# Loading the table places of the supers on TensorE in fours inside the turn instead of sixteen at its head, in a GNN layer kernel

## The chip, the cores and the metric

The kernel runs on one core of one Trainium2 chip. The metric is the device time of one execution in microseconds (us). Engines are named as in the profile: PE is TensorE, DVE is VectorE, ACT is ScalarE, POOL is GpSimd, SP is SyncE, and a name with q (PEldq, SPq) is the sequencer of that engine, which runs register instructions, branches, loads into registers and DMA issues itself.

## The reference, cut to what matters

```python
sums = segment_sum(edge_attr, src, num_segments=n)            # 100000 edges x 64 features into 6250 nodes
counts = segment_sum(ones(edges), src, num_segments=n)
edge_attr_agg = sums / maximum(counts, 1.0)[:, None]
combined = concatenate([x, edge_attr_agg, u[batch]], axis=1)  # batch is all zeros
h = relu(combined @ W1 + b1)
x = layernorm(x + h @ W2 + b2)
```

## The kernel before, in words

The work has three stages. In the first, up to about 450 us, the edges are sorted: PE multiplies each batch of edges by permutation matrices that DVE builds (line 1146), ACT takes the result out of PSUM, and POOL scatters it by an indirect DMA (line 600) into `sorted_rows` in DRAM, grouped by bucket of nodes. Beside it runs the part of the first layer that needs only x.

The second stage, from 452 to 671 us, is the one that the change touches. The sorted rows are read back in 258 "supers" of 128 rows. Each super belongs to one bucket, and its 4 slots are added to that bucket's place in a table that fills all 8 PSUM banks. Per super PE does 24 matmuls (4 slots r, 2 halves h, 3 parts; line 936), each a 128x128 weight load of a one-hot matrix and 64 or 65 columns of data. DVE builds three one-hot matrices of an even super and four of an odd one (line 1236), ACT builds the fourth of the even ones (lines 713 and 716). SP loads the data of two supers with one DMA of 396 KB (line 511) into a ring of 8 pair buffers, once PE has finished with the buffer (`s_added`); it also loads x in 12 pieces (line 527). DVE and ACT write into 4 one-hot buffers, so they can be at most 4 supers ahead of PE; PE waits for them by `s_hot_d` and `s_hot_a` (lines 930 and 932).

Each engine runs its own loop over turns of BODY = 16 supers: 16 turns in a hardware loop (SUP_TURNS, line 942 on PE) and a last straight-line one of 2 supers (line 944). Where in PSUM a super belongs is known only at run time. DVE has computed it, and it lies as 32-bit integers in `where_row`, one row in SBUF: 384 places for PE, then 384 rows of `sorted_rows` for SP. PE's `super_turn` reads the 16 places of its turn into the registers `table_regs` with one load (line 927) at the head of each turn. `snap` (line 929) then turns a register into the address `at` of a super, and the matmuls of line 936 write to `at` and `at + 512`. SP does the same with its own 8 registers at the head of its turn (line 503). These sequencer instructions stand in the same order as the matmuls: PE's sequencer passes weight loads and matmuls on to the engine as it comes to them, and the engine works them off behind it.

The third stage, from 671 us, is the rest of both layers and the norm.

The functions around the change:

Of the kernel before, what the change touches and what calls it, by code (L numbers as in the profile page):

```python
# [9 lines left out]
I32 = mybir.dt.int32  # L10
# [7 lines left out]
P = 128  # L18
# [46 lines left out]
SUPER_PAIRS = -(-SUPERS // 2)  # L65
# [8 lines left out]
SUPER_COLS = -(-SUPERS // P)  # L74
# [20 lines left out]
HOT_BUFS = 4  # L95
BODY = 2 * PAIR_BUFS
SUP_TURNS = SUPER_PAIRS // PAIR_BUFS
ACT_SLOT = SLOTS - 1
TURN = 3
TURNS = CHUNKS // TURN  # L100
# [13 lines left out]
Z_BUFS = 3  # L114
assert X_TURN + X_PIECES + 1 == SUP_TURNS

# [6 lines left out]
def build(nc, x, src, attr, u, w1, b1, w2, b2, out):  # L123
# [12 lines left out]
    with ctx:  # L136
        def sb(name, shape, dt=F32):
            return ctx.enter_context(nc.sbuf_tensor(name, shape, dt))
# [7 lines left out]
        def sem(name):  # L146
            return ctx.enter_context(nc.semaphore(name))

        ident = sb("ident", [P, P])
        b2_all = sb("b2_all", [P, DIM])  # L150
        eps_col = sb("eps_col", [P, 1])
        where_row = sb("where_row", [1, 2 * SUPER_COLS * P], I32)
        node_of = sb("node_of", [P, 2 * P], I16)
        pre = sb("pre", [P, COLS * HID // P * NP])
        stats = sb("stats", [P, 2, 2, 6])
# [248 lines left out]
        def _(sp):  # L404
# [100 lines left out]
            def super_turn(m, count=PAIR_BUFS, found=False):  # L505
                if not found:
                    find_rows(m, count)
                for k in range(count):
                    at = sp.snap(row_regs[k], min_val=0, max_val=ZERO_SUPER * P)
                    sp.wait_ge(s_added, m * BODY + (2 * k + 2))  # L510
                    sp.dma_start(sup_pair[k][:, :, :, :].rearrange("p s r w -> p s (r w)"),
                                 sorted_rows[bass.ds(at, 2 * P), :].rearrange("(s p) w -> p s w", p=P)
                                 ).then_inc(s_sup[k], 16)
# [16 lines left out]
            for lo, hi in ((0, XPART), (XPART, NP)):  # L530
                sp.dma_start(xs[lo:hi, X_PIECES * X_PIECE:COLS * DIM], x_v[lo:hi, X_PIECES * X_PIECE:COLS * DIM]
                             ).then_inc(s_xs, 16)
            super_turn(SUP_TURNS, SUPER_PAIRS - SUP_TURNS * PAIR_BUFS)

# [103 lines left out]
        def _(act):  # L638
# [70 lines left out]
            def super_turn(m, count=BODY):  # L709
                for k in range(0, count, 2):  # L710
                    act.wait_ge(s_sup[k // 2], m * 16 + 16)
                    act.wait_ge(s_added, m * BODY + (k + 1 + SUP_FREE - HOT_BUFS))
                    nc.scalar.activation(apart[k // 2 % 2][:, :], node_of[:, :], ACT.Abs, scale=-1.0,  # L713
                                         bias=place_in[k][:, ACT_SLOT, :]).then_inc(s_apart, 1)
                    act.wait_ge(s_apart, m * PAIR_BUFS + (k // 2 + 1))
                    nc.scalar.activation(onehot[k % HOT_BUFS][:, ACT_SLOT, :], apart[k // 2 % 2][:, :], ACT.Relu, scale=-1.0,  # L716
                                         bias=1.0).then_inc(s_hot_a, 1)

            with act.Fori(0, SUP_TURNS) as m:
                super_turn(m)  # L720
            super_turn(SUP_TURNS, 2 * SUPER_PAIRS - SUP_TURNS * BODY)

# [46 lines left out]
        def _(pe):  # L769
# [153 lines left out]

            table_regs = [pe.alloc_register(f"table_reg{k}") for k in range(BODY)]

            def super_turn(m, count=BODY):
                pe.load(table_regs[0:count], where_row[0:1, bass.ds(m * BODY, count)])
                for k in range(count):
                    at = pe.snap(table_regs[k], min_val=0, max_val=(PAIR_BANKS - 1) * 1024 + (BANK_COLS - 1) * ROW)
                    pe.wait_ge(s_hot_d, m * BODY + (k + 1))  # L930
                    if k % 2 == 0:
                        pe.wait_ge(s_hot_a, m * PAIR_BUFS + (k // 2 + 1))
                    for r in range(SLOTS):
                        for h in range(2):
                            for part, width in ((0, FEAT), (1, FEAT), (2, ROW)):
                                last = nc.tensor.matmul(ps[:, bass.ds(at + h * 512, width)],  # L936
                                                        onehot[k % HOT_BUFS][:, r, h * P:(h + 1) * P],
                                                        sup[k][:, r, part * PLANE:part * PLANE + width],
                                                        start=False, stop=False)
                    last.then_inc(s_added, 1)  # L940

            with pe.Fori(0, SUP_TURNS) as m:
                super_turn(m)
            super_turn(SUP_TURNS, 2 * SUPER_PAIRS - SUP_TURNS * BODY)
            for k in range(BANKS):
                last = nc.tensor.matmul(table_p[k], zeros[:, :], zeros[:, 0:1].to_broadcast([P, table_p[k].shape[1]]),
# [408 lines left out]
```

## Time and profile before

| | us |
|---|---|
| median of 3 runs | 801.06 |
| lowest and highest | 800.24, 801.56 |
| span of the profiled execution, first to last instruction | 799.5 |
| PE busy / DVE busy / ACT busy in the span | 745.1 / 716.8 / 501.7 |

The page gives the span of the profiled execution and no device time of its own for it; the median lies 1.6 us above the span. The matmuls' ends are modelled by the profiler (a matmul of line 936 is shown as 193 ns long, while the next one starts 31 ns after it), so starts are the safer thing to read. A line of a source view gives kind, count, then duration in ns as min/median/max, then the start of the first and of the last one in us.

### The profile page before, as it was taken

The page shows a single profiled execution, that of the slowest core. Times are in us where ns is not written, and L with a number is a line of the kernel's source. Part 1 is how long each engine was busy: PE and PEld are TensorE (multiplying, and loading weights), DVE is VectorE, ACT ScalarE, POOL GpSimd, SP SyncE. Part 2 cuts the span into 40 slices and gives each one's busy share as a digit, 9 for nine tenths or more (in the row PEclk, how much of TensorE's full clock was granted, in tenths as well). Part 3 has the DMA queues.
Part 4 walks back from the last instruction along what each step waited for, and adds up shares of the span by engine and source line. Part 5 has one row for each costly group of instructions (what it writes and reads, how often), then busy time and mean ns, then how long its engine had stood idle before and what let it go on. Part 6 is the DMA issues. An engine that isn't in the chain of part 4 may idle for free.

```text
span 799.5 us, 31269 instructions
## 1 busy us (share of the span) xinstructions
PE 745.1 (93%) x11398; PEld 711.5 (89%) x11399; DVE 716.8 (90%) x2382; ACT 501.7 (63%) x998; POOL 417.1 (52%) x410
## 2 busy tenths in 40 slices
PE   8889999999999999999999888989898986899995
PEld 4689999999999999999999888989898986899995
DVE  8999999999999999999896388989898988799995
ACT  1366676666667767667667545555555552688886
POOL 3087777777677787877776400000000002788983
PEclk9999999999999999999999999999999999999999
DMA  6366556666665666656674678999999990012122
GB/s 215 131 210 204 201 202 211 213 215 219 202 219 195 212 220 211 225 205 214 203 210 167 239 227 260 281 282 282 285 283 285 281 277 10 27 52 64 53 66 64
DMA packets 75268, 156.38 MB, mean 196 GB/s; under 512 B 11084, under 2 KB 51277, under 8 KB 75097
## 3 DMA queue, kind: packets, MB, share of 16 engines
q1 hardware_dynamic: 58328, 102.33, 42.5%
q0 software_dynamic: 16896, 53.54, 17.9%
q8 instruction: 18, 0.29, 0.2%
q14 instruction: 26, 0.20, 0.1%
HBM read 95.47 MB, written 60.37 MB: 195 GB/s over the span
## 4 chain that ended last, share of the span: by engine, by line
PE 60%; DVE 30%; issue 5%; ACT 2%; POOL 1%; DMA 1%; DVEq 0%; ACTq 0%; SPq 0%; POOLq 0%
PE ps L858 33%; DVE onehot L1236 18%; PE ps L785 11%; PE ps L936 5%; PE ps L990 3%; DVE pre L1275 2%; DVE perm L1146 2%; DVE stats L1301 1%; DVE weights_z L1296 1%; PE ps L776 1%; PE ps L792 1%; POOL h_low L628 1%; PE ps L811 1%; PE ps L843 1%; PE ps L841 1%
## 5 line engine op out<-in xcount | busy, mean ns | idle before, releaser
L600 POOL DMA_INDIRECT sorted_rows<-payload,idx x264 | 304.8, 1155 | 131.8 <-issue 51.9
L858 PE MATMUL ps<-attr_buf,perm 128*128 128x198 bf16 x3168 | 302.6, 252 | 1.1 <-ACT attr_buf L642 0.8
L858 PEld LDWEIGHTS ps<-attr_buf,perm 128*128 128x128 bf16 x3168 | 288.6, 96 | 6.1 <-ACT attr_buf L642 1.2
L649 ACT CAST payload<-ps 128x792 bf16<-128x792 f32 x264 | 217.9, 825 | 76.7 <-PE ps L858 62.2
L1146 DVE TENSOR_SCALAR perm<-place_of,pos 128x512 bf16<-128x512 int16 x792 | 241.1, 362 | 3.4 <-PE ps L858 2.7
L1236 DVE TENSOR_SCALAR onehot<-node_of,sup 128x256 bf16<-128x256 int16 x903 | 192.4, 284 | 41.9 <-PE ps L936 22.3
L936 PE MATMUL ps<-sup,onehot 128*128 128x64 bf16 (+1 forms) x6192 | 196.1, 193 | 24.7 <-DVE onehot L1236 21.0
L936 PEld LDWEIGHTS ps<-sup,onehot 128*128 128x128 bf16 x6192 | 193.5, 98 | 27.3 <-issue 27.3
L619 POOL TENSOR_TENSOR xs<-xs,b_all 125x256 f32<-125x256 f32 x50 | 37.6, 775 | 209.4 <-DMA xs<-in_x 209.4
L713 ACT ACTIVATE apart<-node_of,sup 128x256 bf16<-128x256 int16 x129 | 65.6, 508 | 94.3 <-PE ps L936 90.2
L785 PE MATMUL ps<-xt,w1x 128*128 128x125 f32 x800 | 99.9, 278 | 5.9 <-DVE pos L1067 3.3
L785 PEld LDWEIGHTS ps<-xt,w1x 128*128 128x128 f32 x800 | 93.2, 192 | 10.8 <-issue 4.6
L660 ACT ACTIVATE pre<-ps,hid_bias 128x125 f32 (+1 forms) x200 | 56.7, 368 | 61.7 <-PE ps L785 61.7
L628 POOL TENSOR_TENSOR h_low<-pre,h_high 128x500 fp32r<-128x500 f32 x50 | 62.8, 1278 | 32.7 <-ACT pre L737 32.7
L1056 DVE TENSOR_TENSOR attr_buf<-attr_buf 128x576 f32<-128x576 f32 x88 | 65.8, 749 | 7.8 <-DMA attr_buf<-in_edge_attr 7.8
L1062 DVE TENSOR_TENSOR attr_buf<-attr_buf 128x576 f32<-128x576 f32 x88 | 65.4, 744 | 0.0
L716 ACT ACTIVATE onehot<-apart 128x256 bf16<-128x256 bf16 x129 | 53.8, 417 | 4.1
L990 PE MATMUL ps<-w_high,h_high 128*125 128x256 f32 x200 | 49.8, 282 | 1.0 <-issue 0.5
L990 PE MATMUL ps<-w_low,h_high 128*125 128x256 f32 x200 | 49.5, 280 | 0.0
L990 PE MATMUL ps<-w_high,h_low 128*125 128x256 f32 x200 | 34.1, 292 | 7.6 <-POOL h_low L628 7.6
L990 PEld LDWEIGHTS ps<-w_high,h_high 128*125 128x125 f32 x200 | 37.1, 185 | 1.3 <-issue 0.7
L990 PEld LDWEIGHTS ps<-w_low,h_high 128*125 128x125 f32 x200 | 37.2, 186 | 0.0
(150 smaller groups left out, 603.7 us busy)
## 6 DMA issues: line engine op xcount, KB each, us to landing
sup<-sorted_rows SPq DMA_DIRECT2D x129, 396.0 KB, 4.0
attr_buf<-in_edge_attr SPq DMA_DIRECT2D x43, 576.0 KB
out<-weights_z SPq DMA_DIRECT2D x25, 224.0 KB
xs<-in_x SPq DMA_DIRECT2D x12, 448.0 KB
x_stage<-in_x SPq DMA_DIRECT2D x47, 112.0 KB
sorted_rows<-payload,idx POOLq DMA_INDIRECT x264
pre<-jump_d SPq DMA_DIRECT2D x1, 1560.0 KB, 10.4
pre<-first_d SPq DMA_DIRECT2D x1, 780.0 KB, 7.2
```

The source lines that it names most:

```text
L600: pool.indirect_dma_start(out=sorted_rows, out_offset=bass.IndirectOffsetOnAxis(ap=idx[:, n:n + 1], axis=0), in_=payload[s][:, :], in_offs ...
L628: nc.gpsimd.tensor_tensor(h_r[b][1][:, at:end], pre[:, g * KH * NW + at:g * KH * NW + end], h_r[b][0][:, at:end].bitcast(F32), ALU.subtrac ...
L649: nc.scalar.copy(payload[s][:, :].rearrange("p (r w) -> p r w", w=PART), slots_p[s % PSUM_BUFS]).then_inc(s_pay, 1)
L713: nc.scalar.activation(apart[k // 2 % 2][:, :], node_of[:, :], ACT.Abs, scale=-1.0, bias=place_in[k][:, ACT_SLOT, :]).then_inc(s_apart, 1)
L785: last = nc.tensor.matmul(pre_p[b][:, k * NP:(k + 1) * NP], w1x[:, c, k * P:(k + 1) * P], xt[b][:, c, :], start=(c == 0), stop=(c == KX - 1))
L858: last = nc.tensor.matmul(slot_p[s % PSUM_BUFS][r].rearrange("p (h f) -> p h f", f=PLANE), places, parts(a, t * CB + s), start=(t == 0 and ...
L936: last = nc.tensor.matmul(ps[:, bass.ds(at + h * 512, width)], onehot[k % HOT_BUFS][:, r, h * P:(h + 1) * P], sup[k][:, r, part * PLANE:pa ...
L990: last = nc.tensor.matmul(y_p[b][0:NP, c * DIM:(c + 1) * DIM], h_r[b][part][:, at:at + NP], w2r[w_part][:, k * DIM:(k + 1) * DIM], start=( ...
L1056: nc.vector.tensor_tensor(left, whole, high, ALU.subtract).then_inc(s_rest, 1)
L1062: nc.vector.tensor_tensor(low, left, middle, ALU.subtract).then_inc(s_low, 1)
L1146: last = nc.vector.tensor_scalar(perm[s][:, t, :], place_of[:, :], pos[:, bass.ds(c * CT + (t * CB + s), 1)], None, ALU.is_equal)
L1236: last = nc.vector.tensor_scalar(onehot[k % HOT_BUFS][:, r, :], node_of[:, :], place_in[k][:, r, :], None, ALU.is_equal)
```

## The change

PE's 16 places of a turn are no longer read by one load at its head. A function `find_tables` reads 4 of them. Before the loop it is called once for supers 0 to 3. Within a turn of the loop it is called in supers 2, 6, 10 and 14, after the 6 matmuls of their first slot (r == 0), for the four supers that begin two supers later; the call in super 14 reads the first four of the next turn. The last straight-line turn of 2 supers has no load of its own: its places come with the last call in the loop. `where_row` is allocated first in SBUF instead of fourth, so that its address, and those of `ident`, `b2_all` and `eps_col`, are other ones. SP's loads are not changed.

```diff
+PLACES_AT_ONCE = 4
+assert 2 * SUPER_PAIRS - SUP_TURNS * BODY <= PLACES_AT_ONCE
...
+        where_row = sb("where_row", [1, 2 * SUPER_COLS * P], I32)
         ident = sb("ident", [P, P])
         b2_all = sb("b2_all", [P, DIM])
         eps_col = sb("eps_col", [P, 1])
-        where_row = sb("where_row", [1, 2 * SUPER_COLS * P], I32)
...
+            def find_tables(k, at):
+                pe.load(table_regs[k:k + PLACES_AT_ONCE], where_row[0:1, bass.ds(at, PLACES_AT_ONCE)])
+
             def super_turn(m, count=BODY):
-                pe.load(table_regs[0:count], where_row[0:1, bass.ds(m * BODY, count)])
                 for k in range(count):
                     at = pe.snap(table_regs[k], ...)
...
                                                         start=False, stop=False)
+                        if r == 0 and k % PLACES_AT_ONCE == 2 and count == BODY:
+                            following = k - 2 + PLACES_AT_ONCE
+                            find_tables(following % BODY, m * BODY + following)
                     last.then_inc(s_added, 1)
 
+            find_tables(0, 0)
             with pe.Fori(0, SUP_TURNS) as m:
                 super_turn(m)
             super_turn(SUP_TURNS, 2 * SUPER_PAIRS - SUP_TURNS * BODY)
```

## Rows read from the trace of the kernel before

**Rows 1.** The page: its span, and the chain that ended last

```profile
span 799.5 us, 31269 instructions
...
PE 60%; DVE 30%; issue 5%; ACT 2%; POOL 1%; DMA 1%; DVEq 0%; ACTq 0%; SPq 0%; POOLq 0%
```

**Rows 2.** Timeline of PE from 560 to 620 us: turns 8 to 12

```profile
start us, us, engine line op out<-in xcount [idle before <-releaser]
562.64 12.00 PE L936 MATMUL ps<-sup,onehot 128*128 128x64 bf16 x384 [1.30 <-DVE onehot L1236]
575.89 11.99 PE L936 MATMUL ps<-sup,onehot 128*128 128x64 bf16 x384 [1.25 <-DVE onehot L1236]
589.18 11.99 PE L936 MATMUL ps<-sup,onehot 128*128 128x64 bf16 x384 [1.29 <-DVE onehot L1236]
```

**Rows 3.** Busy time by engine in turns 8 and 9

```profile
core 0: us, PE busy (x) PEld busy (x) DVE busy (x) ACT busy (x) POOL busy (x), PEclk, DMA share, GB/s
562.64:575.89 13.25, 12.00 (x384) 11.88 (x385) 11.79 (x56) 7.41 (x16) 0.00 (x0) 1.00 0.95 284
575.89:589.18 13.29, 11.99 (x385) 11.88 (x385) 11.79 (x56) 7.40 (x16) 0.00 (x0) 1.00 0.91 283
```

**Rows 4.** Who waited for whom, 440 to 680 us, and SP's own waits

```profile
engine line waited for: us in total, times, longest us
ACT apart L713 <- PE ps L936: 90.2, 123, 2.4
DVE onehot L1236 <- PE ps L936: 22.3, 17, 1.4
PE ps L936 <- DVE onehot L1236: 21.0, 18, 1.3
PE ps L936 <- ACT onehot L716: 1.6, 1, 1.6
SPq L511 <- PE ps L936: 98.2, 110, 2.2
```

**Rows 5.** Sequencer rows at a turn's head, 573.9 to 576.2 us, by line

```profile
L942 PEldq ALU_OP  x1: 32/32/32, 573.9 to 573.9; - x1
L942 PEldq COMPARE_BRANCH  x1: 207/207/207, 574.0 to 574.0; - x1
L942 PEldq FUSED_REGOPS  x1: 65/65/65, 574.3 to 574.3; - x1
L927 PEldq TENSOR_LOAD <-where_row x1: 1106/1106/1106, 574.4 to 574.4; - x1
L929 PEldq FUSED_REGOPS  x2: 41/41/41, 575.6 to 576.2; - x2
L932 PEldq FUSED_REGOPS  x1: 43/43/43, 575.7 to 575.7; - x1
L936 PEldq FUSED_REGOPS  x2: 43/47/51, 575.8 to 575.9; - x2
```

**Rows 6.** Sequencer rows inside turn 9: supers 4 and 5

```profile
L929 PEldq FUSED_REGOPS  x2: 41/41/41, 578.3 to 579.1; - x2
L936 PEldq FUSED_REGOPS  x2: 37/44/51, 578.5 to 578.7; - x2
```

**Rows 7.** Loads into registers: PE's 17, its last (2), SP's of 8, 8, 1

```profile
L927 PEldq TENSOR_LOAD <-where_row x17: 556/1106/1296, 450.8 to 669.0; - x17
L927 PEldq TENSOR_LOAD <-where_row x1: 556/556/556, 669.0 to 669.0; - x1
L503 SPq TENSOR_LOAD <-where_row x2: 533/536/538, 469.1 to 482.5; - x2
L503 SPq TENSOR_LOAD <-where_row x6: 691/693/697, 563.5 to 629.8; - x6
L503 SPq TENSOR_LOAD <-where_row x1: 507/507/507, 655.8 to 655.8; - x1
```

**Rows 8.** Timeline of PE: turn 0, and turns 15 and 16

```profile
452.46 8.04 PE L936 MATMUL ps<-sup,onehot 128*128 128x64 bf16 x208 [1.58 <-ACT onehot L716]
461.51 3.86 PE L936 MATMUL ps<-sup,onehot 128*128 128x64 bf16 x119 [1.01 <-issue]
466.47 2.03 PE L936 MATMUL ps<-sup,onehot 128*128 128x64 bf16 x57 [1.10 <-issue]
...
655.55 6.87 PE L936 MATMUL ps<-sup,onehot 128*128 128x64 bf16 x216 [1.29 <-DVE onehot L1236]
663.18 0.95 PE L936 MATMUL ps<-sup,onehot 128*128 128x64 bf16 x24 [0.76 <-DVE onehot L1236]
664.84 4.66 PE L936 MATMUL ps<-sup,onehot 128*128 128x64 bf16 x144 [0.70 <-DVE onehot L1236]
669.96 1.69 PE L936 MATMUL ps<-sup,onehot 128*128 128x64 bf16 x48 [0.47 <-DVE onehot L1236]
```

**Rows 9.** Granted clock and matmul count at the start of turn 0

```profile
452.46:455.00 2.54, 2.54 (x51) 2.54 (x52) 1.73 (x9) 0.92 (x2) 0.00 (x0) 0.56 1.04 353
```

## The prediction

> **What bounds the kernel now.** Read the page first: PE and DVE hold 90% of the chain that ended last [rows 1]. The change touches only the stage of supers, so next comes PE's timeline there. Every turn looks alike: 384 matmuls in 12.0 us, then 1.25 to 1.30 us of idle [rows 2]. A matmul starts every 12.0/384 = 0.031 us, a super takes 0.75 us, a turn 13.27 us. From the last matmul's start (its shown end less its 0.19 us) to the next start is 575.89 - (562.64 + 12.00 - 0.19) = 1.44 us, so 1.41 us of each turn are lost at its head.
>
> The view of waits books this to DVE (21.0 us, 18 times), and DVE's idle time to PE (22.3 us, 17 times) [rows 4]: each is said to wait for the other, so a third must hold both. The sequencer's rows show it [rows 5]. PE's sequencer is done with a turn's matmuls at 573.9, half a microsecond before the last of them starts (574.45). Then come the back edge and its register work (to 574.4), the load of 16 places (1.106 us, to 575.54), and three register instructions 0.10 us apart; only then does the first matmul of the turn reach an empty engine, at 575.89. So the head of a turn is bound by PE's sequencer. Elsewhere in it PE bounds: DVE has 11.79 us of work against PE's 12.0 [rows 3], ACT and SP wait for PE [rows 4].
>
> **How far the sequencer runs ahead.** Everything hangs on this. Super 4 of turn 9 starts at 575.89 + 4 x 0.75 = 578.89; its snap runs at 578.3, the next super's at 579.1, again 0.75 us later [rows 6]. So the lead neither grows nor shrinks: about 0.55 us or 17 matmuls, and at the back edge it is 0.5 us again. It is a limit and not the sequencer's pace: restarted at 575.9 with nothing queued, the sequencer had passed 24 matmuls on by 576.2 [rows 5], while some 8 had started, so passing one on takes it some 6 ns and it is soon back at the limit. Whatever holds the sequencer longer than the matmuls still queued becomes idle time of PE.
>
> **Removed.** At 15 turn heads (turns 1 to 15) the load and the 0.058 us behind it: 1.16 us each. The back edge stays, and with it 1.44 - 1.16 = 0.28 us between starts. 15 x 1.16 = 17.5 us. The straight-line turn loses its load of 2, 0.556 us and 0.05 behind it [rows 7]: 0.6. The first load, 1.296 us at 450.8, gets shorter, but the first matmul (452.46) waited for ACT's one-hot too [rows 8]: 0.2. Sum: -18.3 us.
>
> **Added: 64 loads of four.** First the duration. The nearest row is the load of 2 on this very engine, 0.556; SP shows 0.507 for one register and 0.533 to 0.697 for eight [rows 7]. I take 0.58, bounds 0.507 (one register) and 0.697 (eight, the slow ones).
>
> Then what of it shows. Take an even super with a load in it, with super 4's times. Its snap runs at 578.3, its second register instruction of line 936 (the address of h = 1) at 578.7 [rows 6], after three of the first slot's six matmuls. The other three are passed on at once, so the sequencer comes to the new lines at about 578.8. I count one register instruction for the address (0.10, as the others), so the load begins at 578.9, ends at 579.48, and the seventh matmul starts 0.06 later, at 579.54. Undisturbed it starts at 578.89 + 6 x 0.031 = 579.08. The load comes at the worst place: the super's own register work has just eaten 0.4 us of the lead, and only six matmuls have been added. PE stands for 0.46, say 0.47 us. Behind it the other 18 are passed on in a tenth of a microsecond and the lead is back, so each of the four loads of a turn costs the same. The bounds: 0.507 and an address that costs no instruction give 0.30; 0.697 and another 0.05 of register work give 0.63.
>
> Of the 64, two are mostly hidden: in turn 0 the clock is granted at 0.56 (1.2 GHz for nearly all of it) and a matmul takes 2.54/51 = 0.050 us [rows 9], so the queued ones last longer; and in turn 15 PE waits 0.76 and 0.70 us for DVE just before super 10 [rows 8], which a later PE waits less. 62 x 0.47 = +29.1 us.
>
> **Costed at nothing.** The pauses are far from making DVE late: a turn becomes 13.27 - 1.16 + 4 x 0.47 = 13.99 us against its 11.79 [rows 3]. SP's DMAs wait for PE already [rows 4]; if PE goes slower they are asked for later and nothing runs dry. Pauses of half a microsecond are shorter than those of 1.3 us that left the clock at 1.00 [rows 3]. The registers are free (supers 4 to 7 read theirs after super 2), the new places of `where_row`, `ident`, `b2_all` and `eps_col` move no work. The third stage starts later and is not changed. `s_added` comes later only with PE itself.
>
> **The sum.** -18.3 + 29.1 = +10.8 us on a span of 799.5, or, with the 1.6 us around it, on the median of 801.06: **812 us**.
>
> A page of the Trainium skill would say otherwise of the queue. The trace shows some 17 matmuls and their weight loads ahead, 34 instructions. TensorE: Matmul & The Clock Gate (section Architectural detail: the array is 16× 32×32, not 1× 128×128) gives TensorE's queue a depth of 64. That would be 32 matmuls or 1.0 us of lead, the load would hide but for the odd tenth, and this estimate would end at 783 us; the lead in the rows, the same at every super, speaks against it. The time is that of rival 3 below, reached by another road. On the load itself, DMA: Bandwidth & Descriptors (section Latency and other measured facts) gives a floor of about 600 ns per `tensor_load`; the trace goes below it (507 and 556), and with 0.60 the estimate would be 813.
>
> **Rivals.**
> 1. *The load costs more in the stream than the nearest row says* (0.697, as SP's in the middle of its DMAs, and more register work): 0.63 x 62 = 39.1, 822 us. For it: SP's loads of eight took 0.53 early and 0.69 later [rows 7]. Against: its load of one took 0.507 late.
> 2. *The queue is fuller at the load than I read from rows with one decimal.* If the sequencer comes to the load with the full 0.5 us ahead, PE stands for 0.10 + 0.58 + 0.06 - 0.50 - 0.03 = 0.21 us; 62 x 0.21 = 13.0, 796 us. Against: the 0.4 us between snap and second register instruction [rows 6], in which only three matmuls are passed on.
> 3. *Not slower: a load holds up only what reads its registers.* If the sequencer goes on passing matmuls while the four values are on their way, nothing needs them for nearly two supers, 1.3 us, and the loads vanish: 801.06 - 18.3 = 783 us, a turn of 12.11 us, still above DVE's 11.79. It decides from the point where the sequencer takes the next instruction less than about 0.1 us after the load has started. For it: every load in this trace is followed by an instruction that reads its registers, so the 0.06 us between its end and the next one proves nothing [rows 5]. Against: a load is a row of 1.1 us on the sequencer itself, like a branch, and instructions stand there one behind another.
> 4. *The change does not do what it says* (the compiler moves or merges the loads): under 1 in 100; the places are far apart and have matmuls between them.
>
> **How the numbers follow.** The forecast has 0.70, rival 1 0.09, rival 2 0.08, rival 3 0.13. Between the bounds of the stall, 0.30 and 0.63, the forecast runs from 801 to 822. The range takes these, most of rivals 1 and 2, and leaves out rival 3 and the tails: 796 to 824, which holds 0.8. A measurement of this kernel can tell 0.2%, 1.6 us. Within it falls the forecast's lower end (0.30 to 0.32 us a load) and a little of rival 2: 0.05. Faster: rival 3 and most of rival 2, with a little for what I don't see, 0.19. Slower: the rest, 0.76.
>
> **What would show it.** Right: the timeline of PE no longer has runs of 384 matmuls but pauses of 0.3 to 0.6 us after 6 matmuls of every fourth super (54, then 96 apart), the turn's head shows 0.1 to 0.3 us, a turn takes 14.0 us, the source view has 65 loads of about 0.58 us on PE's sequencer. If their duration is right and the pauses are not, the lead was misread; if matmuls are passed on during a load, rival 3 holds and runs of 384 remain. Wrong altogether would be a turn bound by DVE at 11.8 us, or a gap at the head that stays at 1.3 us.

## The result, and the profile after

The changed kernel takes 794.7 us (median of 4 runs, 793.96 to 795.44) against 801.31 us of the kernel before on the same chip: ratio 0.9918, 95% interval 0.9903 to 0.9932. That is 6.6 us faster, where 10.8 us slower was forecast, and 1.3 us below the lower end of the forecast's range (796 to 824).

The page after. Against [rows 1], DVE's share of the chain that ended last has gone from 30% to 11%, and PE has it:

```profile
span 792.2 us, 31365 instructions
...
PE 81%; DVE 11%; issue 2%; ACT 2%; POOL 1%; DMA 1%; ACTq 0%; DVEq 0%; SPq 0%; POOLq 0%
```

Busy time by stage, first of the kernel before, then of the changed one (columns as in rows 3). The stage of supers gives 219.04 - 212.28 = 6.8 of the 7.3 us by which the span is shorter:

```profile
0.00:452.46 452.46, 440.44 (x4348) 414.37 (x4350) 418.56 (x1193) 290.43 (x566) 318.03 (x310) 1.00 0.61 203
452.46:671.50 219.04, 195.91 (x6193) 193.50 (x6194) 191.22 (x898) 118.43 (x256) 4.15 (x6) 0.99 0.86 264
671.50:799.50 128.00, 108.77 (x863) 103.60 (x859) 107.02 (x293) 92.85 (x176) 94.97 (x94) 0.98 0.16 51
```

```profile
0.00:452.52 452.52, 441.03 (x4348) 414.38 (x4350) 419.82 (x1192) 290.29 (x566) 314.89 (x310) 1.00 0.62 203
452.52:664.80 212.28, 205.31 (x6193) 197.37 (x6194) 197.15 (x899) 118.40 (x256) 4.15 (x6) 0.99 0.90 273
664.80:792.20 127.40, 108.83 (x863) 103.42 (x859) 106.06 (x293) 92.83 (x176) 95.17 (x94) 0.97 0.16 51
```

Two turns of the changed kernel, which answer to [rows 3]. A turn takes 12.9 us where it took 13.27:

```profile
558.56:571.46 12.90, 12.63 (x386) 12.14 (x385) 12.15 (x56) 7.45 (x17) 0.00 (x0) 1.00 0.96 292
571.46:584.35 12.89, 12.61 (x385) 12.13 (x385) 12.15 (x56) 7.36 (x17) 0.00 (x0) 1.00 0.97 290
```

PE's timeline over the same kind of stretch as [rows 2]. It no longer breaks at each turn, since the pauses that are left are hardly longer than the 0.19 us for which a matmul is shown. But 1194 matmuls in 40.36 us are not at full pace. Inside a turn of the kernel before, starts are (12.00 - 0.19)/383 = 0.0308 us apart [rows 2]; at that pace the last of the 1194 would end after 37.0 us.

```profile
559.83 40.36 PE L940 MATMUL ps<-sup,onehot 128*128 128x64 bf16 x1194
```

The weight loads, which are shown for only 0.10 us each, still show the pauses, and where they are: 96 matmuls apart (in the third line two stretches run together), that is in every fourth super.

```profile
560.45 3.00 PEld L940 LDWEIGHTS ps<-sup,onehot 128*128 128x128 bf16 x96 [0.16 <-issue]
563.61 3.02 PEld L940 LDWEIGHTS ps<-sup,onehot 128*128 128x128 bf16 x96 [0.16 <-issue]
566.77 6.42 PEld L940 LDWEIGHTS ps<-sup,onehot 128*128 128x128 bf16 x192 [0.15 <-issue]
573.38 3.00 PEld L940 LDWEIGHTS ps<-sup,onehot 128*128 128x128 bf16 x96 [0.18 <-issue]
```

From one matmul's start to the next it is 0.26 us across such a pause (0.24 to 0.31 in turns 4 to 12 of the trace), always behind the sixth matmul of the super. PE loses that less the 0.03 of an ordinary step: 0.23 us a load. At a turn's head starts are now 0.20 us apart (0.18 to 0.22), where it was 1.47.

The waits from 440 to 680 us name the same kind. The mutual waits of PE and DVE [rows 4] have gone from 21.0 and 22.3 us to 1.3 and 2.3; what is new is PE's weight loads idle 52 times, 0.24 us on average, with nobody named:

```profile
DVE onehot L1244 <- DMA sup<-sorted_rows: 16.2, 2, 16.0
PEld ps L940 <- issue: 12.4, 52, 1.6
DVE onehot L1244 <- PE ps L940: 2.3, 6, 0.6
PE ps L940 <- DVE onehot L1244: 1.3, 1, 1.3
```

And the loads themselves, over the whole span. There are 65, as foreseen, with one register instruction each, as counted; but one takes 0.331 us and not 0.58:

```profile
L929 PEldq TENSOR_LOAD <-where_row x65: 328/331/522, 450.8 to 661.5; - x65
L929 PEldq FUSED_REGOPS  x64: 46/46/51, 454.4 to 661.4; - x64
```

### The profile page after: what moved, and what is told of

Read it like the earlier page. It is cut to its first block, busy times and chain, and to the rows that moved or that the text cites. A ratio compares the mean times of both kernels' runs of the same rounds, so it can differ in the third digit from the quotient of the medians.

```text
span 792.2 us, 31365 instructions
## 1 busy us (share of the span) xinstructions
PE 755.2 (95%) x11398; PEld 715.2 (90%) x11399; DVE 723.0 (91%) x2382; ACT 501.5 (63%) x998; POOL 414.2 (52%) x410
## 4 chain that ended last, share of the span: by engine, by line
PE 81%; DVE 11%; issue 2%; ACT 2%; POOL 1%; DMA 1%; ACTq 0%; DVEq 0%; SPq 0%; POOLq 0%
PE ps L860 33%; PE ps L940 26%; PE ps L787 11%; PE ps L998 4%; DVE perm L1154 2%; DVE pre L1283 2%; POOL h_low L630 1%; DVE stats L1309 1%; DVE weights_z L1304 1%; PE ps L794 1%; PE ps L778 1%; PE ps L813 1%; ACT h_high L734 1%; PE ps L845 1%; PE ps L843 1%
## 5 line engine op out<-in xcount | busy, mean ns | idle before, releaser
L602 POOL DMA_INDIRECT sorted_rows<-payload,idx x264 | 301.6, 1143 | 135.2 <-ACT payload L651 52.6
L1244 DVE TENSOR_SCALAR onehot<-node_of,sup 128x256 bf16<-128x256 int16 x903 | 198.2, 285 | 29.6 <-DMA sup<-sorted_rows 16.2
L940 PE MATMUL ps<-sup,onehot 128*128 128x64 bf16 (+1 forms) x6192 | 205.5, 193 | 8.3 <-issue 1.7
L940 PEld LDWEIGHTS ps<-sup,onehot 128*128 128x128 bf16 x6192 | 197.4, 98 | 16.5 <-issue 12.4
```

Source lines behind the costliest of these rows:

```text
L602: pool.indirect_dma_start(out=sorted_rows, out_offset=bass.IndirectOffsetOnAxis(ap=idx[:, n:n + 1], axis=0), in_=payload[s][:, :], in_offs ...
L1244: last = nc.vector.tensor_scalar(onehot[k % HOT_BUFS][:, r, :], node_of[:, :], place_in[k][:, r, :], None, ALU.is_equal)
```

## The experiments

The theory kept from the prediction, called the queue theory below: PE's sequencer waits out a load, and PE stands for as much of it as is longer than the matmuls already queued. Its rivals were that a load halts the engine by itself wherever it stands, that it holds nobody up, and that not the four registers but the new address made it short. Ratios are to runs of the kernel before on the same chip. Time per turn is start to start in the trace. A loss per load is the distance of matmul starts across its pause, as the trace has them in turns 4 to 12, less 0.03 us; where a PE timeline shows the pause as idle time, that distance is the idle time plus the 0.19 us for which a matmul is shown. On the chip of the three kernels from e9 to e11 the whole program was slower (852.5 us for the kernel before, mostly in the first stage), so for these only ratios and turns are used.

**Is it the address?** The change with `where_row` back in its old place, and the kernel before with the new one.

```diff
 # e1_fours_old_place, against the change
-        where_row = sb("where_row", [1, 2 * SUPER_COLS * P], I32)
         ident = sb("ident", [P, P])
         b2_all = sb("b2_all", [P, DIM])
         eps_col = sb("eps_col", [P, 1])
+        where_row = sb("where_row", [1, 2 * SUPER_COLS * P], I32)
 # e2_sixteen_first_place: the same lines the other way round, against the kernel before
```

> The changed kernel, with where_row allocated fourth again, at its old address; everything else as in the change. Theory number (a load of 4 takes 0.33 us because it is 4 registers): loads stay at 0.33 us, pauses at 0.25 us between starts, turn 12.9 us, time 794.7 us as the change. Theory place (the new address made the load short): loads of 0.55 to 0.6 us, pauses of about 0.5 us, turn 13.9 us, time about 810 us.

> The kernel before with where_row allocated first and nothing else changed. Theory number: the load of 16 stays at 1.106 us, turn 13.27 us, time 801.3 us. Theory place: the load gets shorter by a quarter microsecond or more, the 1.44 us between starts at a turn's head with it, and the time falls by 15 times that, 4 us or more, to 797 us or less.

Measured: 796.27 us with fours at the old place (ratio 0.9922, 0.9901 to 0.9942), turns of 12.9 us; 802.44 us with sixteens at the new one (1.0003, 0.9988 to 1.0018), turns of 13.27 us. The loads between 590 and 640 us, of the first and of the second:

```profile
L929 PEldq TENSOR_LOAD <-where_row x16: 328/332/341, 590.3 to 638.7; - x16
```

```profile
L927 PEldq TENSOR_LOAD <-where_row x3: 1104/1111/1120, 602.0 to 628.5; - x3
```

The move in SBUF does nothing here. At either place every four starts a multiple of 16 bytes behind the row's start (the row's own address is in no trace); what a shift by 4 bytes does is below.

**Does the place in the super matter?** The same loads after the second and after the third slot.

```diff
-                        if r == 0 and k % PLACES_AT_ONCE == 2 and count == BODY:
+                        if r == 2 and k % PLACES_AT_ONCE == 2 and count == BODY:   # e4; r == 1 in e5
```

> The change with the same loads after the third slot (r == 2, 18 matmuls into the super) and not after the first. Queue theory: by then the lead is full again at about 0.5 us, the address and the load hold the sequencer for 0.10 + 0.33 + 0.06 us, so the pauses all but vanish (under 0.05 us), a turn takes 12.1 us, time 794.7 - 62 x 0.22 = about 781 us. Rival (a load makes the engine stand for a time of its own, wherever it is, or drains it): pauses stay at 0.25 us and the time at 795 us. Second rival (DVE becomes the bound): pauses vanish but the time stops at about 785 us, with PE waiting for one-hots.

> The change with its loads after the second slot (r == 1, 12 matmuls into the super). Queue theory: 6 more matmuls are queued than after the first slot, 0.19 us, for some 0.03 us of passing on, so of the 0.22 us that PE loses per load about 0.06 are left: between the change and the third slot, near the latter, ratio to before 0.983 (788 us on 801.3). Rival (a slot's place acts only at the super's border): no different from the first slot, ratio 0.992.

Measured: third slot 785.03 us, ratio 0.9787 (0.9765 to 0.9809); second slot 785.39 us, ratio 0.9808 (0.9785 to 0.983). Both intervals lie far below the change's. Two turns with the third slot, and its PE timeline:

```profile
555.44:567.59 12.15, 12.15 (x386) 12.05 (x385) 11.80 (x57) 7.40 (x17) 0.00 (x0) 1.00 0.99 305
567.59:579.73 12.14, 12.14 (x386) 12.04 (x385) 11.82 (x57) 7.44 (x17) 0.00 (x0) 1.00 0.98 309
```

```profile
559.83 40.36 PE L940 MATMUL ps<-sup,onehot 128*128 128x64 bf16 x1272
```

In the same 40.36 us there are now 1272 matmuls, 0.0317 us each, and a turn is 12.14 us. Of these 11.8 are 384 steps at the ordinary pace; starts are 0.17 us apart at the turn's head, and behind the third matmul of the super after each load they are 0.06 apart once (0.05 to 0.09), 0.03 more than ordinary. At the load itself there is no gap. With the second slot a turn is

```profile
554.11:566.43 12.32, 12.30 (x385) 12.14 (x385) 11.88 (x56) 7.45 (x17) 0.00 (x0) 1.00 0.96 306
```

and starts are 0.11 us apart at the load. So a load costs PE 0.23 us after the first slot, 0.08 after the second, and 0.03 after the third, the last one super later. The turns agree: (12.90 - 12.14)/4 = 0.19 and (12.32 - 12.14)/4 = 0.05 us a load more than in the third place. The same load, with the same duration, costs PE three different amounts by what is queued ahead of it. A load that halts or drains the engine is excluded, and so is one that holds nobody up. DVE, with 11.8 us of work a turn, did not become the bound. The third slot gives the fastest version here, about 784 us on the scale of the 801.3. That is 3 us more than expected: the queue theory had left no cost per load, and 62 x 0.03 = 2 us of it are the 0.03.

**Moved but not split, and split but not moved.**

```diff
 # e7_sixteen_moved, against the change
-PLACES_AT_ONCE = 4
+PLACES_AT_ONCE = 16
-                        if r == 0 and k % PLACES_AT_ONCE == 2 and count == BODY:
-                            following = k - 2 + PLACES_AT_ONCE
-                            find_tables(following % BODY, m * BODY + following)
+                        if r == 0 and k == BODY - 1 and count == BODY:
+                            find_tables(0, m * BODY + BODY)
 # e10_fours_at_head, against the change: no loads inside the turn, and at its head
+                for k in range(0, count, PLACES_AT_ONCE):
+                    find_tables(k, m * BODY + k)
```

> Moved but not split: one load of 16 for the next turn, after the first slot of super 15. Queue theory: the load holds the sequencer for 0.10 + 1.106 + 0.06 us against 0.3 us of matmuls still queued; PE loses 0.9 to 1.0 us there, and the turn's head keeps the 0.14 us of the back edge: a turn of 13.1 us against 13.27 before and 12.9 in the change, ratio 0.996. If splitting is what pays and moving nothing, the turn stays at 13.3 us, ratio 1.00.

> Split but not moved: four loads of 4 at each turn's head, none inside. If a load's time is 0.07 + 0.065 us a register whoever reads the registers next, the four take 1.33 us and their register work 0.2 to 0.4: the head gets 0.4 to 0.6 us worse than before, ratio 1.01. If splitting alone makes loads cheap (they overlap each other), the head shrinks below 1.2 us and the ratio is under 0.995.

Measured: moved, ratio 0.9934 (0.9914 to 0.9954), a turn of 12.95 us; split at the head, ratio 1.0167 (1.0116 to 1.0217), a turn of 14.0 us. PE's timelines:

```profile
560.51 11.71 PE L940 MATMUL ps<-sup,onehot 128*128 128x65 bf16 x367
572.94 12.22 PE L940 MATMUL ps<-sup,onehot 128*128 128x64 bf16 x384 [0.72 <-issue]
585.90 1.27 PE L940 MATMUL ps<-sup,onehot 128*128 128x64 bf16 x27 [0.74 <-issue]
```

```profile
626.57 12.01 PE L942 MATMUL ps<-sup,onehot 128*128 128x64 bf16 x384 [2.01 <-issue]
640.54 12.04 PE L942 MATMUL ps<-sup,onehot 128*128 128x64 bf16 x384 [1.96 <-issue]
654.54 12.00 PE L942 MATMUL ps<-sup,onehot 128*128 128x64 bf16 x384 [1.96 <-issue]
```

Moving the whole load into the stream gives 0.32 of the change's 0.38 us a turn, and the two ratios overlap within their intervals. Splitting costs: four loads of 0.33 and their register work are longer than one of 1.11. It pays only where each quarter falls under matmuls of its own that are queued, and after the first slot these are too few: four losses of 0.23 us are as much as the one of 0.89 (0.73 + 0.19 - 0.03) in e7. (The expectation for e10 was 0.4 to 0.6 us more at the head; it was 0.7. Four of its turns take 15.2 to 15.5 us, at a granted clock of 0.89 to 0.91 where the others have 1.00; that adds 5.6 us to what the split costs, 0.7% in the ratio.)

**How long is a load, by its size?** Eights, twos and ones after the first slot, and eights after the third.

```diff
 # e3_eights, e11_eights_third_slot
-PLACES_AT_ONCE = 4
+PLACES_AT_ONCE = 8
 # e6_twos: PLACES_AT_ONCE = 2, in every even super
+                        if r == 0 and k % 2 == 0 and count == BODY:
+                            following = k + 2
+                            find_tables(following % BODY, m * BODY + following)
 # e9_ones: PLACES_AT_ONCE = 1, in every super
+                        if r == 0 and count == BODY:
+                            find_tables((k + 2) % BODY, m * BODY + (k + 2))
```

> The change with 8 places per load: two loads a turn, in supers 2 and 10, after the first slot. The queue theory (PE stands for the load's time less about 0.11 us) with a load that grows by some 0.03 us a register gives loads of about 0.45 us, pauses of 0.34 us lost each, 0.68 us a turn against 0.88 with fours: about 791 us. If a load of 8 takes 0.53 to 0.7 us, as SyncE's do, it is 0.42 to 0.6 us lost twice a turn, 794 to 799 us.

> Loads of 8 (0.59 us) after the third slot, two a turn. Queue theory with a full lead of 0.5 us: the sequencer is held for 0.10 + 0.59 + 0.06 us, PE loses about 0.2 us each, 0.4 us a turn: ratio 0.987 against 0.979 with fours there and 0.995 with eights after the first slot.

> The change with 2 places per load, in every even super after the first slot, 8 loads a turn. Line through 4, 8 and 16 registers (0.33, 0.59, 1.106 us: 0.07 + 0.065 a register): 0.20 us a load, held against the lead PE loses about 0.09 each, 0.7 us a turn against 0.88: ratio 0.989. Floor theory (nothing under 4 registers is cheaper; the load of two at the end of the kernel before took 0.556): loads of 0.33 to 0.56 us, 0.22 to 0.45 us lost 8 times a turn, ratio 1.01 to 1.04.

> One place per load, in every super after the first slot, 16 loads a turn. Line theory: 0.135 us a load, nearly hidden, ratio about 0.98 to 0.985. Floor theory (SyncE's load of one took 0.507 us): a load of 0.33 to 0.5 us in each super, 3.5 to 6 us lost a turn, ratio 1.04 to 1.08.

Measured: eights 0.9951 (0.993 to 0.9972); eights after the third slot 0.9874 (0.9826 to 0.9922); twos 1.0432 (1.0407 to 1.0457), 836 us, with turns of 15.6 us; ones 1.0396 (1.0332 to 1.046), turns of 15.3 us. Their loads, 590 to 640 us, in the order eights, twos, ones:

```profile
L929 PEldq TENSOR_LOAD <-where_row x7: 587/589/594, 595.1 to 634.1; - x7
```

```profile
L929 PEldq TENSOR_LOAD <-where_row x25: 534/539/552, 591.3 to 638.2; - x25
```

```profile
L928 PEldq TENSOR_LOAD <-where_row x53: 296/301/329, 590.0 to 639.8; - x53
```

Two registers take longer than four, and the expectations by a line through 4, 8 and 16 fell with that: twos were to be better than fours and are worse by 42 us. The eights took 0.59 us and not the 0.45 of their first reading, and their time is the second one's. PE's timeline, first with eights, then with twos:

```profile
563.42 6.04 PE L940 MATMUL ps<-sup,onehot 128*128 128x64 bf16 x192 [0.36 <-issue]
569.78 6.28 PE L940 MATMUL ps<-sup,onehot 128*128 128x64 bf16 x192 [0.32 <-issue]
```

```profile
566.79 1.64 PE L940 MATMUL ps<-sup,onehot 128*128 128x64 bf16 x48 [0.26 <-issue]
568.73 1.63 PE L940 MATMUL ps<-sup,onehot 128*128 128x64 bf16 x48 [0.30 <-issue]
```

Eights lose 0.50 us a load, twos 0.44. Eights after the third slot came as the queue theory has it:

```profile
602.17:614.78 12.61, 12.45 (x386) 12.17 (x385) 11.98 (x57) 7.40 (x17) 0.00 (x0) 1.00 0.98 299
```

At the load starts are 0.26 us apart, so 0.23 are lost there; at the start of the next super another 0.06.

**By what rule?** The row of places shifted by one element, and each four loaded as three and one.

```diff
 # e12_fours_off_by_one: the row has 8 elements more, is filled from element 1, SP reads one further on too, and
             def find_tables(k, at):
+                at = at + 1
                 pe.load(table_regs[k:k + PLACES_AT_ONCE], where_row[0:1, bass.ds(at, PLACES_AT_ONCE)])
 # e13_three_and_one
-                pe.load(table_regs[k:k + PLACES_AT_ONCE], where_row[0:1, bass.ds(at, PLACES_AT_ONCE)])
+                pe.load(table_regs[k:k + 3], where_row[0:1, bass.ds(at, 3)])
+                pe.load(table_regs[k + 3:k + 4], where_row[0:1, bass.ds(at + 3, 1)])
```

> The change with the whole row of places shifted by one element (4 bytes) in SBUF, so that no group of four starts at a multiple of 16 bytes. Piece theory (a load is done in pieces of about 0.26 us, and a piece is four registers only if they lie in one aligned 16 bytes, else one): 4 pieces, 1.0 to 1.1 us a load, pauses of 1.0 us, a turn of 16 us, ratio about 1.05. Without the alignment clause: 0.33 us as before, ratio 0.992. A load that touches two aligned 16 bytes costs two pieces: 0.59 us, ratio 1.01.

> The change with each load of four made as a load of three and a load of one. Piece theory (registers that do not fill a four are loaded singly): 0.78 us and 0.30 us, with their register work a pause of 1.1 to 1.2 us, a turn of 16.5 us, ratio about 1.06. Rival (a load costs by the aligned 16 bytes it touches, and loads of one and two were long for another reason): 0.33 and 0.30 us, a pause of 0.6 to 0.7 us, a turn of 14.6 us, ratio about 1.025.

Measured: off by one 1.0443 (1.0424 to 1.0461), turns of 15.6 us; three and one 1.063 (1.0611 to 1.065), turns of 16.5 us. The loads of each, then PE's timeline of the first:

```profile
L930 PEldq TENSOR_LOAD <-where_row x13: 998/1002/1017, 590.9 to 637.6; - x13
```

```profile
L929 PEldq TENSOR_LOAD <-where_row x12: 774/778/781, 591.9 to 637.5; - x12
L930 PEldq TENSOR_LOAD <-where_row x12: 307/310/313, 592.8 to 638.4; - x12
```

```profile
580.41 3.09 PE L941 MATMUL ps<-sup,onehot 128*128 128x64 bf16 x96 [0.73 <-issue]
584.23 3.11 PE L941 MATMUL ps<-sup,onehot 128*128 128x64 bf16 x96 [0.73 <-issue]
```

The same four values take 0.33 us from the old start and 1.00 us from 4 bytes beside it. A start 8 bytes beside it was not tried, so that 16 bytes are the measure is what the expectations supposed and not shown. All sizes on PE now fit two formulas. Taken in fours: 0.07 + 0.26 us per four (0.33, 0.59, 1.11). Taken singly: 0.06 + 0.24 us per register (0.30, 0.54, 0.78 for one, two, three, and 1.02 for four, measured 1.00). SyncE shows it too: its loads of 8 in e12, 0.53 to 0.70 us unshifted [rows 7], take 1.67 to 1.85 in the stage, and its load of one is as short as before (0.495 us):

```profile
L505 SPq TENSOR_LOAD <-where_row x17: 495/1838/2230, 432.4 to 688.4; - x17
```

**The cover, from all of them.** A load of D holds the sequencer for D + 0.16 us (0.10 for its register instruction, 0.06 after it). What of this PE does not lose is the cover: the time that the matmuls already queued last. After the first slot of an even super: fours 0.33 + 0.16 - 0.23 = 0.26 us; eights 0.59 + 0.16 - 0.50 = 0.25; twos 0.54 + 0.16 - 0.44 = 0.26; fours off by one 1.00 + 0.16 - 0.90 = 0.26. So loads from 0.33 to 1.00 us have the same cover. After the second slot it is 0.33 + 0.16 - 0.08 = 0.41; after the third, from the eights and at the load alone, 0.59 + 0.16 - 0.23 = 0.52 us, which is about the full lead of [rows 6]. An odd super has less register work at its start and more cover: in super 15, e7 gives 1.11 + 0.16 - 0.89 = 0.38. The ones show the difference within one kernel, 0.25 us lost in even supers (cover 0.21) and 0.15 in odd ones (0.31). Both are 0.05 to 0.07 us below the others, so with a load in every super the lead is not quite back at the next.

**One that told nothing.**

```diff
 # e8_fours_twice, against the change
                             find_tables(following % BODY, m * BODY + following)
+                            find_tables(following % BODY, m * BODY + following)
```

> The change with each load in the turns issued twice in a row, the same four places again. Queue theory (nothing of a second load is hidden): each pause grows by 0.33 us and its register work of 0.06 to 0.1, to 0.65 us between starts, a turn takes 14.5 us and the time rises by 25 to 27 us over the change: ratio 1.024. Rival (the sequencer does not wait for a load, the pause has another cause): the pause grows by 0.1 us or less, ratio at most 1.00.

Measured: 794.6 us, ratio 0.992 (0.9897 to 0.9942). Its trace has 65 loads and 64 register instructions as the change's:

```profile
L929 PEldq TENSOR_LOAD <-where_row x65: 328/332/518, 450.1 to 661.1; - x65
```

So one load of each pair must have been dropped in building (nobody reads the values of the first). It is a repeat of the change, and speaks neither for nor against a theory. The dose that it was to give comes from fours, eights and off-by-one fours instead: 0.33, 0.59 and 1.00 us of load cost 0.23, 0.50 and 0.90 us.

## Why the prediction was wrong

**The bound, the lead and the removed part held.** PE's own sequencer bound the turn's head; with the load gone the mutual waits of PE and DVE vanished. The lead of 17 matmuls, read from rows with one decimal, is in the whole trace of the kernel before: in turns 1 to 15 the register instruction at each super's start but a turn's first stands 17 matmuls ahead of the engine (224 of 225 times, once 16). What stays at the head was put at 0.28 us between starts and is 0.20: the removed part was 0.08 us a turn too small, 1.2 us in all; where that went was not tried. The sequencer passed 21 matmuls on between 575.97 and 576.16, so 9 ns each and not 6; no term of the sum hangs on it.

**The mechanism of the added part held.** Pauses after the sixth matmul of supers 2, 6, 10 and 14, no overlap with later matmuls, the lead back before the next load: all as described. The trace has the load of turn 9's super 2 start at 573.00 and end at 573.35, and the seventh matmul start at 573.41, 0.06 behind it. The working gave PE's loss as the load's duration less 0.12 us (0.58 to 0.46), that is a cover of 0.10 + 0.06 + 0.12 = 0.28 us; the runs show 0.25 to 0.26.

**The step that failed is the duration of a load of four.** I took 0.58 us, near the load of two (0.556), between bounds of 0.507 and 0.697. It is 0.33, below the lower bound. With it, and nothing else changed, the sum is 62 x (0.33 - 0.12) - 18.3 = -5.3 us, 796 us: the sign and most of the size. With the loss of a load and the turn's head as measured it is 62 x 0.23 - 18.3 - 1.2 = -5.2 us, since these two small misses cancel. The other 1.4 of the measured 6.6 us are in no term; most of them are in turn 0 (below). The error lay in the choice of the nearest row. I treated the load as a fixed cost with little per register, because one register on SyncE and two on PE cost about the same; but these were loads of single registers, a kind of their own, and the only row of the kind at hand was the load of 16: four fours in 1.106 us [rows 7]. A quarter of it is 0.28 us, which I did not write down as a bound. A smaller load being the dearer one was never considered, so "bounds from the nearest rows" covered only one side.

**The rivals.** Rival 1 (a dearer load) fell: in the stream, with DMAs running, four registers take 0.328 to 0.354 us in the changed kernel. Rival 2 had nearly the right time (796) by the wrong road: the queue was not fuller than read (0.26 us of cover, not 0.5). Rival 3 fell with the change itself, and harder with e7 and e12: a load of 1.11 or 1.00 us shows up as a pause of nearly that, though the first reader of its registers is 18 matmuls (e7) or more than a super (e12) behind. Rival 4 did not happen in the change, whose trace has its 65 loads where the program puts them.

The Trainium skill's page TensorE: Matmul & The Clock Gate (section Architectural detail: the array is 16× 32×32, not 1× 128×128) gives TensorE's queue a depth of 64, from which the prediction estimated 1.0 us of lead. In no place here did more than 0.52 us hide, so the rows decide. The Trainium skill's page DMA: Bandwidth & Descriptors (section Latency and other measured facts) gives about 600 ns as the floor of a `tensor_load`; the loads here go down to 0.30 us.

**What is left unexplained.** Turn 0 became 1.4 us shorter (17.3 to 15.9 us); the terms of the sum, one head less three loads, give 0.6 of it. It has pauses with no releaser named in both kernels (1.01 and 1.10 us before [rows 8]), and it is 16.4 us long in e8, whose trace has the same loads, so I give this no cause. It counts towards the 6.8 us of the stage: turns 1 to 14 are 5.4 of them, and turn 15 and the straight-line turn gave nothing (together 15.9 us in the kernel before, 16.0 in the changed one), a load of two less and three pauses more being about even.

## What to carry to other kernels

A register load on the sequencer is paid by the engine only as far as it outlasts what is queued. Put it where the queue is fullest, here behind the third slot and not behind the first, whose super has just spent the lead on its own register work: that alone took the gain from 0.8% to 2.1%. On this engine load registers in fours, from a start that keeps their alignment: two cost more than four, and one element of shift triples the price. When a cost is read from the nearest row, ask first whether that row is of the same kind; an interpolation between unlike ones can miss from outside its own bounds.

## What the runs showed of the hardware that I had not expected

- The time of a load into registers is no function of their number alone: on PE 0.30, 0.54, 0.78, 0.33 us for 1, 2, 3, 4, then 0.59 for 8, 1.11 for 16, and 1.00 for 4 that start 4 bytes further on.
- The first load of PE in each kernel is 0.19 us longer than the others of its size: 1.296 against 1.106 in the kernel before, 0.522 against 0.331 in the change. It is not the constant address: with ones the second load ahead of the loop has one too and takes 0.308 us, and with fours at the head the first load stands inside the loop and takes 0.514. Why the first is longer stays open.
- The lead lost to a load is won back within about a super: with four loads a turn after the third slot starts are nowhere behind a load more than 0.09 us apart, and that only at the start of the next super.
